# Four instead of two buffers of six edge tiles for the count rows of a graph network, and VectorE's split of a weight half placed ahead of its weighing

## What is computed

```
seg = dst * num_rel + etype
sums = segment_sum(x[src], seg)
cnt = segment_sum(ones, seg)
mean = sums / maximum(cnt, 1.0)
out = einsum('nri,rio->no', mean, W) + x @ root + b
```

## Time and profile before

| what | value |
|---|---|
| median of 3 runs | 2232.96 us (2224.12 to 2234.2) |
| the profiled execution's own time | 2233.14 us |
| its span in the profile | 2231.4 us |
| TensorE busy | 1944.1 us (87%) |
| VectorE busy | 1220.8 us (55%) |
| ScalarE busy | 836.4 us (37%) |
| GpSimd busy | 555.6 us (25%) |
| mean granted TensorE clock | 0.950 of full |

### The profile page before, as it was taken

One profiled execution on the slowest core, in us unless ns is written; L12 is line 12 of the kernel. 1 busy time (PEld: TensorE's weight loads), 2 busy tenths in 40 slices (PEclk: granted clock), 3 DMA queues, 4 the chain that ended last, 5 costly groups with the idle time before them and its releaser, 6 DMA issues.

```text
span 2231.4 us, 34620 instructions
## 1 busy us (share of the span) xinstructions
PE 1944.1 (87%) x11158; PEld 1701.2 (76%) x11159; DVE 1220.8 (55%) x2255; ACT 836.4 (37%) x1123; POOL 555.6 (25%) x538
## 2 busy tenths in 40 slices
PE   6988888989999989689999999996779768768887
PEld 5888786759999967479999999994449756656565
DVE  7941213554444654665555655544555776565775
ACT  2221222332222223235555555553333246431665
POOL 0004745640000056444344333103660000000000
PEclk9999999999999999989999999997999979879999
DMA  5545567853556477557788888875871021100111
GB/s 169 156 150 153 146 161 252 272 174 125 164 168 200 159 237 251 167 178 259 269 274 273 280 263 270 275 231 186 266 246 36 1 63 41 57 33 25 54 50 51
DMA packets 204058, 378.40 MB, mean 170 GB/s; under 512 B 18971, under 2 KB 174412, under 8 KB 203962
## 3 DMA queue, kind: packets, MB, share of 16 engines
q1 hardware_dynamic: 171306, 246.23, 34.2%
q0 software_dynamic: 31216, 128.89, 18.2%
q10 hardware_dynamic: 1440, 1.97, 0.2%
HBM read 288.68 MB, written 88.34 MB: 169 GB/s over the span
## 4 chain that ended last, share of the span: by engine, by line
PE 68%; DVE 10%; issue 6%; DMA 6%; ACT 4%; POOL 2%; another core or an unknown queue 2%; ACTq 1%; SPq 0%; DVEq 0%; POOLq 0%
PE ps L1837 40%; PE ps L1719 6%; PE ps L2054 4%; PE ps L1714 3%; PE ps L1694 3%; PE ps L2019 2%; DMA arena<-in_L_gnn_W_rel 2%; POOL arena L528 2%; PE ps L1866 2%; DMA arena<-U,ix 2%; PE ps L2090 1%; PE ps L1639 1%; ACT arena L838 1%; PE ps L1980 1%
## 5 line engine op out<-in xcount | busy, mean ns | idle before, releaser
L1837 PE MATMUL ps<-w_hi,hT_hi 128*128 128x384 f32 x2052 | 722.8, 352 | 54.3 <-issue 20.1
L1837 PE MATMUL ps<-w_lo,hT_hi 128*128 128x384 f32 x2052 | 696.4, 339 | 0.4 <-issue 0.4
L1837 PE MATMUL ps<-w_hi,hT_lo 128*128 128x384 f32 x2052 | 696.4, 339 | 0.3 <-issue 0.3
L1837 PEld LDWEIGHTS ps<-w_hi,hT_hi 128*128 128x128 f32 x2052 | 393.5, 192 | 64.6 <-issue 30.1
L1837 PEld LDWEIGHTS ps<-w_lo,hT_hi 128*128 128x128 f32 x2052 | 393.5, 192 | 1.2 <-issue 1.0
L528 POOL DMA_INDIRECT arena<-U,ix x252 | 272.4, 1081 | 485.9 <-DMA U<-arena 369.6
L1837 PEld LDWEIGHTS ps<-w_hi,hT_lo 128*128 128x128 f32 x2052 | 392.6, 191 | 0.5 <-issue 0.5
L614 ACT ACTIVATE arena<-ps 128x384 f32<-128x384 f32 x160 | 78.2, 491 | 464.2 <-PE ps L1837 392.7
L1719 PE MATMUL ps<-arena,onehot 128*128 128x512 f32 x504 | 195.2, 511 | 19.9 <-DVE onehot_r L1079 7.6
L953 DVE TENSOR_TENSOR w_lo<-arena,w_hi 128x2304 fp32r<-128x2304 f32 x45 | 114.9, 2555 | 134.1 <-ACT w_hi L607 106.6
L1719 PEld LDWEIGHTS ps<-arena,onehot 128*128 128x128 f32 x504 | 90.3, 197 | 97.6 <-issue 93.3
(11 more groups left out here) (282 smaller groups left out, 2959.2 us busy)
## 6 DMA issues: line engine op xcount, KB each, us to landing
arena<-in_L_gnn_W_rel SPq DMA_DIRECT2D x74, 1152.0 KB, 6.2
U<-arena SPq DMA_DIRECT2D x292, 192.0 KB
arena<-in_L_gnn_W SPq DMA_DIRECT2D x36, 1152.0 KB
U<-z SPq DMA_DIRECT2D x28, 864.0 KB
arena<-rows_d SPq DMA_DIRECT2D x42, 320.0 KB, 3.4
arena<-in_L_gnn_root SPq DMA_DIRECT2D x4, 1152.0 KB
arena<-U,ix POOLq DMA_INDIRECT x252
arena<-in_L_gnn_W_root SPq DMA_DIRECT2D x2, 1152.0 KB
```

What stands on the lines that cost most here:

```text
L1837: ins = pe.matmul(acc, l, r[:, j, kt, :], start=(n == 0), stop=(n == 3 * KT - 1))
```

## The change

There are four buffers for groups of six tiles in place of two (`KR = 4`). The loops over groups are written out on GpSimd and VectorE, GpSimd takes its row numbers from `ix` directly, and `ixb`, its copy and its wait are gone. GpSimd may now be four groups ahead of the weighing. VectorE's order in turns 4 to 7 is: split, then (from the second half on) weigh two groups, those whose number is two less than in the order before; the last split of turn 7 is followed by groups 12 and 13. A semaphore for another table (`urow_st`) is merged into `kinv_st`.

```
+KR = 4
-        kgat = counts[:]...[:, NT * P // 2:NT * P // 2 + GU * (R0 + R1)].rearrange("p (b n) -> p b n", b=GU)
+        kgat = counts[:]...[:, NT * P // 2:NT * P // 2 + KR * GB * (R0 + R1)].rearrange("p (b n) -> p b n", b=KR * GB)
-        ixb = sb("ixb", [P, GU], I32)
...
-            def indices(table, it, j, k):
-                pool.tensor_copy(ixb[:, j:j + GB], ix[:, table, ds(GU * it + j, GB)]).then_inc(S["pool_idx"], 1)
-                pool.wait_ge(S["pool_idx"], NT // GB * k + 2 * it + j // GB + 1)
-                pool.sem_inc(S["nop"], 1)
...
-            with pool.Fori(0, NT // GU) as it:
-                for j in range(GU):
-                    if j % GB == 0:
-                        pool.wait_ge(S["w_done"], 2 * it + j // GB + 1)
-                        indices(2, it, j, 0)
-                    pool.indirect_dma_start(out=kgat[:, j, :], ..., ap=ixb[:, j:j + 1], axis=0)).then_inc(k_in[j // GB], 16)
-            pool.wait_ge(S["w_done"], NT // GB + 2)
+            for q in range(NT // GB):
+                pool.wait_ge(S["w_done"], q + 1)
+                for t in range(GB * q, GB * (q + 1)):
+                    pool.indirect_dma_start(out=kgat[:, t % (KR * GB), :], ..., ap=ix[:, 2, t:t + 1], axis=0)).then_inc(k_in[q % KR], 16)
+            pool.wait_ge(S["w_done"], NT // GB + KR)
...
-                    with dve.Fori(4, lo) as it:
-                        for j in range(2):
-                            split(it, o + j + 1)
-                            for k in range(2):
-                                weigh(2 * it - 8 + j, k)
-                    for it in range(lo, nr):
-                        pair(it, False)
+                    for n in range(2 * (nr - 4)):
+                        split(4 + n // 2, o + n % 2 + 1)
+                        for q in range(2 * n - 2, 2 * n):
+                            if q >= 0:
+                                weigh(q)
-                    for k in range(2):
-                        weigh(NT // GU - 1, k)
-                    dve.wait_ge(S["w_done"], NT // GB + 2)
+                    dve.wait_ge(S["w_done"], NT // GB + KR)
...
-            dve.sem_inc(S["w_done"], 2)
+            dve.sem_inc(S["w_done"], KR)
```

More of the change, by code:

```diff
@@ L118, in gnn_kernel @@
         oh_all = rad[:, 0:NT * P].rearrange("p (t n) -> p t n", t=NT)
-        kgat = counts[:].rearrange("p a g n -> p (a g n)")[:, NT * P // 2:NT * P // 2 + GU * (R0 + R1)].rearrange(
-            "p (b n) -> p b n", b=GU)
+        kgat = counts[:].rearrange("p a g n -> p (a g n)")[:, NT * P // 2:NT * P // 2 + KR * GB * (R0 + R1)].rearrange(
+            "p (b n) -> p b n", b=KR * GB)
         oh_r = gat.rearrange("p b n -> p (b n)").bitcast(F16)[:, 0:NT * (R0 + R1)].rearrange("p (t n) -> p t n", t=NT)
@@ L236, in gnn_kernel @@
             "x_dma edges_in nop w64_in consts vec_ok ln_var ln_std ln_h hT_tp hT_hi hT_lo "
-            "w_hi w_first w_lo steps evac pool_idx msg_oh msg_hi msg_lo agg_pe acc_out "
+            "w_hi w_first w_lo steps evac msg_oh msg_hi msg_lo agg_pe acc_out "
             "srt_rs srt_ps srt_rhs srt_mm srt_tab cnt_oh cnt_pe k_inv kinv_st w_pr w_done "
-            "key_ok key_tp ov_ok urow_st urow_ok u_zero l_oh l_pe l_ix h_st hc_tp hc_hi hc_lo "
+            "key_ok key_tp ov_ok urow_ok u_zero l_oh l_pe l_ix h_st hc_tp hc_hi hc_lo "
             "v_in v_hi v_lo v_mm v_ev "
@@ L248, in gnn_kernel @@
         v_st = [sem(f"v_st{j}") for j in range(2)]
-        k_in = [sem("k_in0"), sem("k_in1")]
+        k_in = [sem(f"k_in{j}") for j in range(KR)]
         g_in = [sem(f"g_in{b}") for b in range(RB)]
@@ L360, in phase @@
                     sp.wait_ge(S["key_ok"], 2)
-                    sp.dma_start(urow_d.rearrange("(r n) o -> r (n o)", n=NP), urow).then_inc(S["urow_st"], 16)
+                    sp.dma_start(urow_d.rearrange("(r n) o -> r (n o)", n=NP), urow).then_inc(S["kinv_st"], 16)
                     lo = NT // 18 + 1
@@ L532, in _ @@
             pool.wait_ge(S["kinv_st"], 16)
-            with pool.Fori(0, NT // GU) as it:
-                for j in range(GU):
-                    if j % GB == 0:
-                        pool.wait_ge(S["w_done"], 2 * it + j // GB + 1)
-                        indices(2, it, j, 0)
-                    pool.indirect_dma_start(out=kgat[:, j, :], out_offset=None, in_=kinv_d,
-                                            in_offset=bass.IndirectOffsetOnAxis(ap=ixb[:, j:j + 1], axis=0)).then_inc(k_in[j // GB], 16)
-            pool.wait_ge(S["w_done"], NT // GB + 2)
+            for q in range(NT // GB):
+                pool.wait_ge(S["w_done"], q + 1)
+                for t in range(GB * q, GB * (q + 1)):
+                    pool.indirect_dma_start(out=kgat[:, t % (KR * GB), :], out_offset=None, in_=kinv_d,
+                                            in_offset=bass.IndirectOffsetOnAxis(ap=ix[:, 2, t:t + 1], axis=0)).then_inc(k_in[q % KR], 16)
+            pool.wait_ge(S["w_done"], NT // GB + KR)
             for g in range(NG):
@@ L552, in _ @@
             pool.wait_ge(S["hT_tp"], 3 * KT)
-            pool.wait_ge(S["urow_st"], 16)
+            pool.wait_ge(S["kinv_st"], 32)
             def urow_out(b):
-                pool.wait_ge(k_in[b % 2], 16 * GB * (NT // GU + b // 2 + 1))
+                pool.wait_ge(k_in[b % 2], 16 * GB * (-(-NT // (GB * KR)) + b // 2 + 1))
                 pool.tensor_copy(ix[:, 3, GB * b:GB * (b + 1)], urow_g[:, GB * (b % 2):GB * (b % 2 + 1)]).then_inc(S["urow_ok"], 1)
@@ L754, in _ @@
             phase(Q_C1, R0, ST_C1)
-            act.wait_ge(S["w_done"], NT // GB + 2)
+            act.wait_ge(S["w_done"], NT // GB + KR)
             messages_root(0, Q_C2)
@@ L1039, in counted, with weigh @@
                 dve.reciprocal(kinv[:], kinv[:]).then_inc(S["k_inv"], 1)
[L1041 to L1045, removed]
+            def weigh(q):
+                kg = kgat[:, GB * (q % KR):GB * (q % KR + 1), :]
+                t = slice(GB * q, GB * (q + 1))
+                dve.wait_ge(k_in[q % KR], 16 * GB * (q // KR + 1))
                 dve.tensor_tensor(kg, kg, oh_r[:, t, :], ALU.mult).then_inc(S["w_pr"], 1)
-                dve.wait_ge(S["w_pr"], 2 * it + j + 1)
+                dve.wait_ge(S["w_pr"], q + 1)
                 dve.tensor_reduce(wgt[:, 0, t], kg[:, :, 0:R0], AX.X, ALU.add)
@@ L1292, in phase @@
                     counted()
-                    lo = 4 + NT // GU // 2
-                    with dve.Fori(4, lo) as it:
-                        for j in range(2):
-                            split(it, o + j + 1)
-                            for k in range(2):
-                                weigh(2 * it - 8 + j, k)
-                    for it in range(lo, nr):
-                        pair(it, False)
+                    for n in range(2 * (nr - 4)):
[3 more added lines that the diff above has]
+                                weigh(q)
                     lo = nr
-                    for k in range(2):
-                        weigh(NT // GU - 1, k)
-                    dve.wait_ge(S["w_done"], NT // GB + 2)
+                    dve.wait_ge(S["w_done"], NT // GB + KR)
                 if lo < nr:
```

## The result

The changed kernel takes 2255.49 us (median of 15 runs) beside 2233.06 us for the kernel before (15 runs on the same chip): ratio 1.0092, 95% interval 1.0067 to 1.0117. That is 22.4 us slower, outside the predicted 2210 to 2244. The profiled execution takes 2265.91 us with a span of 2263.9.

What follows compares the result with a forecast made beforehand. TensorE was taken to bound the kernel, idling for late signals beside the gathers. VectorE's order and the copies counted 0 and GpSimd's new position 3.5 us, off 2233.14 us: 2229.6 us, range 2210 to 2244.

Steps and rivals of the forecast that it cites:

- The stage, the lost 28 to 36 us and the chain through remote waits: 190 to 316 us, count-row gathers: TensorE loses 28 to 36 us, waiting for ScalarE evacs whose TensorE signals come late.
- The signal whose lateness was put at some 5 us: TensorE's completion signal for the evac at 206.03 us, said to reach ScalarE some 5 us late.
- VectorE's order, 0: VectorE's splits and weighings: one split 9.9 us earlier, waits for gathered rows mostly gone, nobody waiting behind them: worth 0.
- issue early and wait late: Skill rule on transfers: VectorE's 52.1 us of waits would go, worth 0, or 9.9 us at most.
- GpSimd's copies ... The direct worth is 0.: GpSimd's gather groups: removing copy and wait saves 0.7 us for each of 14, 10 us, but nobody waits: 0.
- Where GpSimd stands next: GpSimd with four buffers: held 5 us ahead of group 10, until 297.4 ahead of group 12; worth 3.5 us to TensorE.
- The 1.1 us that I took from the gathers' end to the signal: ScalarE's last remote wait ends 1.1 us behind the last gather; the same delay was assumed in the hold before group 12.
- remote waits over 70 us: Sign of being wrong: ScalarE's remote waits in the stretch with gathers rising above 70 us, from 60.0 before.
- Slower, the pauses were what let signals through: Rival: without 13 pauses between gather groups, three or four waits last longer, plus 9 to 20 us; about 2243, chance 0.17.
- the signal of 214.58: TensorE's signal releasing ScalarE's evac at 214.58 us without a GpSimd pause, cited against the slower rival.
- Nothing moves: Rival: the price hangs on the 84 gathers, wherever they lie; time 2233 us, chance 0.16.
- a matmul's end is an estimate: Skill rule: late signals may be matmuls really ending late, slowed by gathers; the gain is then 0, not 3.5 us.

Runs made afterwards that it cites:

- g_third: The changed kernel with a GpSimd copy, waited for, ahead of every gather, on chip 4: 2216.16 us, ratio 0.9921 to the kernel before.
- after_third: The changed kernel, nothing altered, run as control on chip 13: 2192.33 us, ratio 0.9970 to the kernel before.
- after_fourth: The changed kernel, nothing altered, run again as control on chip 4: 2255.68 us, ratio 1.0105 to the kernel before.
- after: The changed kernel as first measured, against the kernel before: 2255.49 us, ratio 1.0092.
- c_order: The changed kernel with VectorE's order of before put back, four buffers and no copies, on chip 4: 2268.80 us, ratio 1.0180 to the kernel before.
- b_again: The changed kernel with one copy, waited for, put back per six gathers, on chip 15: 2194.58 us, ratio 0.9968 to the kernel before.

## Why the prediction was wrong, point by point

- *The stage, the lost 28 to 36 us and the chain through remote waits* were read rightly. The signal whose lateness was put at some 5 us reached the semaphore 5.9 us late, and the next one 11.4. `g_third` gains 2233.66 - 2216.16 = 17.5 us against before with the late signals nearly gone, and still pays 11 to 14 us of GpSimd's time for its copies (by chip 13).
- *VectorE's order, 0.* The waits for gathered rows went and were worth nothing, as said. But the order is not neutral: at two groups of buffers it gave 11.9 us, at four 2268.80 - 2255.49 = 13.3 us. With the old order 36 and 48 gathers go out before the first hold, with the new one 24 and 36. That the shorter first run is what the order gains is likely, not shown. I had looked only at who waits for VectorE, not at what VectorE's weighing releases. The rule of the Trainium skill to issue early and wait late (page "DMA: Bandwidth & Descriptors", section "Rules for kernel authors") bought nothing through the waits it speaks of: 52.1 us of them fell to 7.5.
- *"GpSimd's copies ... The direct worth is 0."* **This is the step that failed.** Where signals are held, removing the copies, the 0.8 us behind them and the loops costs 27.3 us, of which the forecast had nothing. Where none are, the change gains 7.5 to 8.5 us, and the likely reason fails the same step the other way: GpSimd's issue is on the path there (the first message waits for it in `after_third`), so the 10 us of copies count. No trace of the kernel before was taken on such a chip, so this share is not shown. The 35.97 us in which GpSimd waits for stores in the earlier trace rows are cover only because TensorE's halves are late.
- *"Where GpSimd stands next", holds of 5 us and 4.4 us ahead of groups 10 and 12.* Measured: 17.38 us ahead of group 6, then 8.64, 8.80 and 8.60. I took the times of VectorE's splits from the trace of before and held them fixed, though a split waits for the very signals that the gathers hold. The right count closes the loop: 15 us for twelve gathers, 2.4 until the signal, then 6.2 for the evacs, `w_hi`, split and weighing: 23.3 and 23.5 us a half measured. The 1.1 us that I took from the gathers' end to the signal was 2.4 there. The sign that I named for being wrong, remote waits over 70 us, came (79.5 over all the gathers; up to 316 us it is 59.1), but it is a rough one: `after_fourth` is as slow with 52.1, since the profile puts some held signals down to TensorE itself.
- *"Slower, the pauses were what let signals through", 2243 at 0.17.* The nearest of the rivals, mis-sized and with too little of the chance: 9 to 20 us less 3.5 was put for three or four waits that last to the next opening. The lateness does not end at the next opening, it grows from step to step, and one wait alone grew to 24.8 us. The evidence against it, the signal of 214.58 that came without a pause, was read as if pauses were the only way through. Signals do come without them, 11.4 us late in that case.
- *"Nothing moves", the price hangs on the 84 gathers.* Wrong: the same 84 gathers cost 22 us more or less by the gaps between them. The Trainium skill's rule that a matmul's end is an estimate (page "Perfetto Trace Analysis", section "Tensor Engine Instruction") does not reach this far. The signal of the matmul that ends at 214.04 came at 241.62, and behind that matmul TensorE had issued the 18 of the next step, whose own signal followed within 0.17 us, where the steps of `after_third` end 3.12 us apart. So the lateness lies behind the matmuls and not in their execution; whether the acknowledgement or the signal behind it is held, no run here tells.
- *The chip.* All numbers of the prediction came from a trace with late signals. I had not thought of a chip without them.

**Open.** Why chips 13 and 15 hold nothing; each ran in one set only, so a state that passes is not ruled out. Whether, on chip 4, the length of one break counts or the mean rate of the gathers: about 1 us per six gathers there (one every 1.37 us on average) gives the kernel before its 44 to 60 us of remote waits, 0.48 per six (1.28) gives 64, 0.47 after each (1.44) gives 8.8. Two readings speak for the rate. The lateness grows along a run, and after a longer run the signals need longer to come: 2.4 us behind the last of twelve gathers, 4.7 behind the last of 36 (`after`), 5.9 behind the last of 48 (`c_order`). That looks like something that piles up faster than it is cleared and not like a door that opens in breaks, but no run tests it. Breaks after two or three gathers ran on hold-free chips alone, and two copies per six only on chip 5. So the kernel with a copy ahead of each gather (`g_third`) is the best version measured on chip 4 (0.9921), the changed kernel as it stands on chips 13 and 15, with `b_again` and a copy per three gathers too near to tell from it; a break after every third gather costs 1.5 to 1.8 us on these two and is untried on chip 4.

## What to carry to other kernels

A pause on an engine that nobody waits for can still be what keeps others running; before removing one, ask what it leaves room for. Where a trace puts waits down to "remote" on a single core, look at which engine's signals are late and who issues indirect DMAs back to back at the time, and count forward only with the loop closed: the consumer's times move with what delays them. And repeat a change of under 1% on a second chip: here the sign of the result went with the chip.

## What the runs showed of the hardware that had not been expected

- While GpSimd issues gathers of small rows, 0.94 us each with 0.30 us between them, TensorE's completion signals come ever later on chip 4: up to 27.6 us in `after`, 35.7 in `c_order`. They catch up 2.4 us after a run of twelve gathers and 4.7 after one of 36. ScalarE's signals arrive at once in the same stretch: with gathers going on, the split starts at 202.38 where `w_hi` ends at 202.34, and the matmul at 216.94 where the evac ends at 216.89. 0.47 us between any two gathers end it nearly (8.8 us of remote waits left).
- Chips differ in it: remote waits of 52.1 to 79.5 us in the same program on chip 4, none on 13 and 15. Between 960 and 1500 us too, evacs of the changed kernel have 33.1 us of them on chip 4 (`after_fourth`) and none on chip 13 (`after_third`).
- The kernel before takes 2233.7 us on chip 4, 2215.5 on chip 5 and 2200 on the others: a spread of 1.5% in one program, more than the change.
